# TensorE's program of a spline stage: 32 chunks written out, or a loop over two chunks with its wait counts in registers

## The reference

```
w1b, w2b = sign(w1), sign(w2)
out = relu(batchnorm(conv3x3(x, w1b), gamma1, beta1))
x   = relu(batchnorm(conv3x3(out, w2b), gamma2, beta2) + x)
u = (clip(x * a + b, -1.5, 1.5) + 1) * 0.5 * (K - 1)
i, t = floor(u), u - floor(u)
spline = sum over 4 neighbours of alpha_table[i + k] * basis_k(t)       # R = 8 numbers
out = id_gain * x + einsum('bchwr,cr->bchw', spline, mix) + bias
```

## Time and profile before

| what | value |
|---|---|
| median of 3 runs | 1164.68 us (1160.93 to 1167.83) |
| profiled execution, its own time | 1162.34 us |
| its span, first to last instruction | 1160.5 us |
| mean granted TensorE clock | 0.981 |
| TensorE, weight loads, DVE, ACT busy | 94%, 65%, 82%, 78% |
| first matmul of the spline stage | 445.28 us |
| last 128 matmuls of TensorE (T_LIN and T_VAL of chunk 31) | from 1146.05 us, 5.49 us |

### The profile page before, as it was taken

One profiled execution on the slowest core, in us unless ns is written; L12 is line 12 of the kernel. 1 busy time (PEld: TensorE's weight loads), 2 busy tenths in 40 slices (PEclk: granted clock), 3 DMA queues, 4 the chain that ended last, 5 costly groups with the idle time before them and its releaser, 6 DMA issues.

```text
span 1160.5 us, 51486 instructions
## 1 busy us (share of the span) xinstructions
PE 1093.0 (94%) x23818; PEld 751.4 (65%) x23818; DVE 954.2 (82%) x891; ACT 909.4 (78%) x451; POOL 138.6 (12%) x219
## 2 busy tenths in 40 slices
PE   6999999699999946999999999999999999999996
PEld 4678888578888833665666656665656766665664
DVE  5855656585665777999999999999999999999987
ACT  4435443678788627999999999999999999999971
POOL 7000000058000000011010110110110101101100
PEclk9999999899999977999999999999999999999998
DMA  6766765667767766899999989989999999999652
GB/s 229 260 257 256 278 241 224 229 236 279 278 256 281 289 249 169 189 218 228 220 218 230 218 214 236 220 216 237 215 220 222 213 230 212 225 217 219 147 134 85
DMA packets 58225, 260.95 MB, mean 225 GB/s; under 512 B 16336, under 2 KB 16336, under 8 KB 50000
## 3 DMA queue, kind: packets, MB, share of 16 engines
q1 hardware_dynamic: 48880, 209.20, 55.7%
q0 software_dynamic: 8640, 48.17, 22.7%
q10 hardware_dynamic: 544, 1.10, 0.3%
HBM read 104.29 MB, written 77.07 MB: 156 GB/s over the span
## 4 chain that ended last, share of the span: by engine, by line
PE 60%; DVE 1%; issue 1%; ACTq 0%; ACT 0%; DVEq 0%
PE tab L1161 52%; PE tab L1170 8%; ACTq L949 0%; DVE lin L1120 0%; DVE poly L1116 0%; DVE zbuf L1024 0%; DVE lin L1012 0%; DVE far_sq L1085 0%; DVE poly L1091 0%; DVE middle_mask L1046 0%; ACT zbuf L933 0%; ACT cell L941 0%; DVE lin L1018 0%; DVE offset L1032 0%; DVEq L1084 0%
## 5 line engine op out<-in xcount | busy, mean ns | idle before, releaser
L1161 PE MATMUL tab<-edge_mask,diag 128*32 128x392 bf16 x10240 | 446.8, 329 | 5.9 <-issue 5.9
L1161 PEld LDWEIGHTS tab<-edge_mask,diag 128*32 128x32 f16 x10240 | 277.1, 97 | 168.9 <-issue 28.4
L981 ACT ACTIVATE edge_mask<-cell,thr 128x6272 bf16<-128x6272 bf16 x62 | 338.6, 5508 | 0.5 <-DMA cell<-cell 0.5
L414 ACT ACTIVATE yout<-acc 128x1568 f32<-128x1568 f32 x64 | 94.2, 1472 | 163.0 <-PE acc L715 140.8
L1161 PE MATMUL tab<-middle_mask,diag 128*32 128x392 bf16 x4096 | 186.9, 332 | 26.8 <-DVE middle_mask L1046 22.9
L715 PE MATMUL acc<-band_split,w 64*64 64x392 f16 x4608 | 198.6, 330 | 9.9 <-ACT band_split L372 6.5
L715 PE MATMUL acc<-split,w 64*64 64x392 f16 x4608 | 196.5, 330 | 11.2 <-DVE w L467 9.7
L715 PEld LDWEIGHTS acc<-band_split,w 64*64 64x64 f16 x4608 | 164.3, 107 | 44.0 <-issue 14.8
L715 PEld LDWEIGHTS acc<-split,w 64*64 64x64 f16 x4608 | 154.5, 107 | 52.4 <-issue 11.8
L1161 PEld LDWEIGHTS tab<-middle_mask,diag 128*32 128x32 f16 x4096 | 110.3, 98 | 91.5 <-DVE middle_mask L1046 23.0
L524 DVE BATCH_NORM_STATS2 stats<-yout 128x392 f32 (+1 forms) x240 | 118.0, 555 | 60.8 <-ACT yout L414 60.0
(11 more groups left out here) (133 smaller groups left out, 956.2 us busy)
## 6 DMA issues: line engine op xcount, KB each, us to landing
y_scratch<-yout SPq DMA_DIRECT2D x32, 1568.0 KB, 6.2
cell<-cell SPq DMA_DIRECT2D x504, 98.0 KB, 5.0
xin<-y_scratch SPq DMA_DIRECT2D x16, 1568.0 KB, 9.1
lin<-far POOLq DMA_DIRECT2D x32, 784.0 KB, 9.5
out<-lin SPq DMA_DIRECT2D x31, 784.0 KB, 5.6
xin<-in_x SPq DMA_DIRECT2D x15, 1568.0 KB, 9.3
lin<-y_scratch SPq DMA_DIRECT2D x30, 784.0 KB, 9.5
lin<-in_x POOLq DMA_DIRECT2D x28, 784.0 KB, 7.7
```

Of the source, the lines that this page charges most:

```text
L414: act.activation(yout[b][:, :].rearrange("p (r k x) -> p k r x", r=2, k=TILES)[:, 2 * part:2 * part + 2], acc[:, 4 * part:4 * part + 4, 0: ...
L981: act.activation(mask_of(c, q)[:, :, :], cell4[c % 2][:, :, :], ACT.Sign, bias=thr[:, q:q + 1]).then_inc(sign_mask_ready, 1)
L1161: mm = pe.matmul(tab[(c + t) % 2][j * GROUP:(j + 1) * GROUP, sub, 0:SUB], keep["diag"][part][:, j % 2, t, q, :], mask_of(c, q)[:, j, sub * ...
```

## The change

Only TensorE's program of the spline stage is rewritten. Chunks 0 and 1 are written out, then a loop of 14 rounds runs over two chunks each (an even and an odd one, since the buffers alternate), and chunks 30 and 31 are written out again. The matmuls, their order and the counts they wait for stay the same. In the loop the counts depend on the loop's variable, so they are worked out in registers.

```diff
-            def product(c, t, q, sub):
+            def product(odd, t, q, sub):
+
+                masks = edge_mask[odd][EDGE_QUADS.index(q)] if q in EDGE_QUADS else mask_of(odd, q)
...
             def wait_for_mask(c, q):
 
-                if c == 0:
+                if isinstance(c, int) and c == 0:
                     pe.wait_ge(mask_ready, QUAD_ORDER.index(q) + 1)
                 elif q in EDGE_QUADS:
-                    pe.wait_ge(sign_mask_ready, edge_masks(c - 1) + EDGE_QUADS.index(q) + 1)
+                    pe.wait_ge(sign_mask_ready, len(EDGE_QUADS) * (c - 1) + EDGE_QUADS.index(q) + 1)
                 else:
-                    pe.wait_ge(mask_ready, dve_masks(c - 1) + MIDDLE_QUADS.index(q) + 1)
-
-            def table(c, t):
+                    pe.wait_ge(mask_ready, len(QUAD_ORDER) + len(MIDDLE_QUADS) * (c - 1) + MIDDLE_QUADS.index(q) + 1)
+
+            def table(c, odd, t):
 
                 wait_past(pe, table_used, used(c, t) - 2)
...
-            for c in range(CHUNKS):
-                for t in range(TABLES):
-                    table(c, t)
+            def two_chunks(i):
+                for odd in range(2):
+                    for t in range(TABLES):
+                        table(2 * i + odd, odd, t)
+
+            two_chunks(0)
+            with pe.Fori(1, CHUNKS // 2 - 1) as i:
+                two_chunks(i)
+            two_chunks(CHUNKS // 2 - 1)
```

More of the change, by code:

```diff
@@ L1156, in _ @@
         def _(pe):
-            def product(c, t, q, sub):
+            def product(odd, t, q, sub):
+                masks = edge_mask[odd][EDGE_QUADS.index(q)] if q in EDGE_QUADS else mask_of(odd, q)
                 for part in range(2):
                     for j in range(4):
-                        mm = pe.matmul(tab[(c + t) % 2][j * GROUP:(j + 1) * GROUP, sub, 0:SUB],
+                        mm = pe.matmul(tab[(odd + t) % 2][j * GROUP:(j + 1) * GROUP, sub, 0:SUB],
                                        keep["diag"][part][:, j % 2, t, q, :],
-                                       mask_of(c, q)[:, j, sub * SUB:(sub + 1) * SUB],
+                                       masks[:, j, sub * SUB:(sub + 1) * SUB],
                                        start=(q == QUADS_OF[t][0] and part == 0),
@@ L1166, in product, with add_near_part @@
                 return mm
-            def add_near_part(c, sub):
-                return pe.matmul(tab[(c + T_SQ) % 2][:, sub, 0:SUB], keep["ident"][:, :],
-                                 poly[c % 2][:, sub * SUB:(sub + 1) * SUB], start=False, stop=True)
+            def add_near_part(odd, sub):
+                return pe.matmul(tab[(odd + T_SQ) % 2][:, sub, 0:SUB], keep["ident"][:, :],
+                                 poly[odd][:, sub * SUB:(sub + 1) * SUB], start=False, stop=True)
             def wait_for_mask(c, q):
-                if c == 0:
+                if isinstance(c, int) and c == 0:
                     pe.wait_ge(mask_ready, QUAD_ORDER.index(q) + 1)
                 elif q in EDGE_QUADS:
-                    pe.wait_ge(sign_mask_ready, edge_masks(c - 1) + EDGE_QUADS.index(q) + 1)
+                    pe.wait_ge(sign_mask_ready, len(EDGE_QUADS) * (c - 1) + EDGE_QUADS.index(q) + 1)
                 else:
-                    pe.wait_ge(mask_ready, dve_masks(c - 1) + MIDDLE_QUADS.index(q) + 1)
-            def table(c, t):
+                    pe.wait_ge(mask_ready, len(QUAD_ORDER) + len(MIDDLE_QUADS) * (c - 1) + MIDDLE_QUADS.index(q) + 1)
+            def table(c, odd, t):
                 wait_past(pe, table_used, used(c, t) - 2)
-                if c == CHUNKS - 1 and t == T_VAL:
+                if isinstance(c, int) and c == CHUNKS - 1 and t == T_VAL:
                     for sub in range(4):
                         for q in QUADS_OF[t]:
-                            mm = product(c, t, q, sub)
+                            mm = product(odd, t, q, sub)
                         mm.then_inc(table_ready, 1)
@@ L1198, in table @@
                     for sub in range(4):
-                        mm = add_near_part(c, sub)
+                        mm = add_near_part(odd, sub)
                 mm.then_inc(table_ready, 1)
-            for c in range(CHUNKS):
-                for t in range(TABLES):
-                    table(c, t)
+            def two_chunks(i):
[6 more added lines that the diff above has]
+            two_chunks(CHUNKS // 2 - 1)
 def build(nc, x, w1, w2, par_dram, mix_t, alpha_t, out):
```

## The result

The changed kernel takes 1268.91 us (median of 4 runs, 1265.22 to 1279.12), the kernel before 1164.74 us beside it: 1.091 times as long, 95% interval 1.084 to 1.098, 104 us more.

A forecast was written before the change was run, and what follows sets the result against it. The prediction took TensorE, 94% busy, as the bound. From the profiled 1162.3 us: -13.4 fetch stalls, +62 misses, +8 clock = 1219, forecast 1221 us as a median; 8 in 10 range 1188 to 1315 us.

The forecast's parts named there:

- the likeliest case: Spline loop on TensorE: one missing block per round, 13 times 4.8 us, forecast 1221 us, chance 0.35.
- the second rival: Every block of the spline loop is given up in turn; with two stalls a round median 1295 us, chance 0.25.
- Does the body fit?: The spline loop's 1842 instructions touch 8 blocks, a ninth is fetched too, and nine were taken not to fit.
- That the one given up is the oldest, the loop's first: The ninth block's fetch pushes out the spline loop's first block, giving one miss per round, 62 us in 13.
- The 13.4 us of fetch stalls: TensorE's idle time for late code blocks, chunks 4 to 30 of the spline stage; forecast removed, -13.4 us.
- The price of a miss: At each taken spline-loop branch: 5.7 us latency plus 0.2 branch less 1.1 queued, 4.8 us (1.6 to 7.2).
- The second miss: In the second rival, the next block, 55 instructions after the loop's start, also misses: 4.6 us each, 60 us more.
- The clock: TensorE restarting at half speed after stops: 2.6 us each, 33 us for 13; a quarter counted, 8 us.
- Registers, the moved wait: Spline loop's register operations and the sequencer's own wait for `table_used`: costed at nothing; uncovered, register operations would be 8 us.
- taken branches of the fitting loop: 13 taken branches closing the spline loop on TensorE, at 0.17 us each: +2.2 us.
- The fitting loop: Rival: the spline loop's code stays held and nothing is fetched again; median 1153 us, chance 0.14.

The follow-up runs named there:

- e_less_loop: Changed kernel without the products of T_VAL's low halves: loop body of 1714 instructions touching 7 blocks, no hint; 1146.86 us, ratio 0.985 to the kernel before.
- e_less_slot: As e_less_loop, the same 1714 instructions, but the loop starts 200 instructions into a block and touches 8 blocks; 1262.21 us, ratio 1.083 to the kernel before.
- e_hint: Changed kernel plus one hint instruction per round at the loop's top, naming the closing branch as likely taken; 1154.37 us, ratio 0.992 to the kernel before.
- e_slot0: Changed kernel with the loop's first instruction placed on the edge of a 256-instruction block, still touching 8 blocks; 1257.10 us, ratio 1.079 to the kernel before.
- e_stop_long: e_hint with the loop placed on a block's edge and an empty 16-round loop on TensorE's sequencer ahead of each two chunks; 1260.96 us, ratio 1.083.
- e_once: Changed kernel with its loop replaced by fourteen one-round loops, all chunks written out; wait counts came out as constants; 1161.24 us, ratio 0.998 to the kernel before.
- e_hint_last: e_hint with the hint's outcome read from a register, likely in rounds 1 to 13, unlikely in the last; 1147.85 us, ratio 0.987 to the kernel before.

## Why the prediction came out as it did

The direction was right, and the time lies in the range (1221 us forecast, 1268.9 measured, 1188 to 1315), but the likeliest case was not the one that happened: 56 us more were forecast and 104 came. The range holds the result only because it had been stretched for the second rival. That is partly luck: that rival's 1295 us is near because its second stop was taken far too dear (60 us, measured 18) and its clock too cheap (8 us, measured 29).

*Does the body fit?* Right as argued: eight blocks touched, a ninth asked for, nine too many. e_less_loop and e_less_slot show the limit from both sides, e_hint that the ninth fetch is the cause. The Trainium skill ("Runtime: NRT & Kernel Launch", Instruction fetch mechanics) gives TensorE 2048 instructions in blocks of 256, which is eight; all three runs agree. The same section's sentence that only two blocks are held doesn't: e_less_loop repeats seven without a fetch.

*"That the one given up is the oldest, the loop's first"*: this is the step that failed, in what I let follow from it. I took it that only this one is lost in a round. Nine packets come in every round, so all eight are lost. It was my second rival, the case of two stalls, for which I had 1295 us and a chance of 0.25. That each fetch gives up the oldest block, and so the next one that is needed, explains the nine; that a missing target empties the whole memory would give nine as well, and no run tells the two apart. The 13.4 us of fetch stalls, which the forecast took off, stayed: 12.4 us of idle in place of 9.8.

*The price of a miss.* 4.8 us forecast; measured 53.7 / 13 = 4.1 us of idle, 4.3 in pace. The 5.7 us of latency and 0.2 of branch in it were 5.1 together. This term was mis-sized by little, and the row of one bad block and the share of late ones bracketed it well.

*The second miss.* 4.6 us forecast for that rival, 0.9 us of idle measured, 1.4 in pace; e_slot0 shows that it is one. I had the fetch begin when the loop is entered and take 5.7 us again. In the trace its packet starts 0.8 us behind the end of the branch (592.00, the branch ends at 591.22), where the first miss's starts 2.4 us behind the branch's start, and the matmul behind the second stop starts 2.7 to 3.5 us behind the branch's end. And at half clock the 27 matmuls ahead of it last up to 2.2 us in place of 1.1.

*The clock.* 8 us for the likeliest case. 13 falls came, one at each long stop, and they cost 2.2 us each, 29 us; e_stop_long has 2.3 without any fetch. A quarter of the falls was too few, 2.6 us apiece a little too much: the upper end of 33 us was nearly it.

*The sum by measured terms* is taken from the two traces: the distance of each matmul of the spline stage to the next, less what it is in an undisturbed chunk. 13 x 4.3 (first stop) + 13 x 1.4 (second) + 13 x 2.2 (clock) + 3 (more at the other edges) = 106 us, and the two profiled executions are 1268.1 - 1162.3 = 105.8 us apart. Nothing of the loss is left over.

*Registers, the moved wait.* Nothing, as forecast, which e_hint shows and e_once doesn't. The 2.2 us for taken branches of the fitting loop weren't there either (43.04 us a round).

*The fitting loop.* 1153 us forecast for it; e_hint takes 1154.4 us and has one miss at its end, e_hint_last 1147.9.

## What to carry to other kernels

Count a loop's instructions, and the 256-instruction blocks that they touch from where the loop starts, and add the block behind the end: here TensorE kept eight in all (no run looked at another engine's limit), and one more turned a loop that saves 15 us into one that costs 104. If a body is near that, a hint for its closing branch, or a shift of its start so that it touches a block less, decides it, and the count of code packets in the profile tells at once which side one is on. Before shortening the busiest engine's work, look whether a chain through another engine has the same period. And when a test takes a mechanism apart, look in its trace whether the instructions that it is to test are still there.

## What the runs showed of the hardware that I had not expected

- With nine blocks for eight places every block is fetched again in each round (9 packets), not only the one that is over.
- A hint on the closing branch changes what is fetched ahead: 117 packets fewer, branches of 0.22 us in place of 5.07, and one stop of 4.97 us where the loop falls through, which a hint with a register's outcome removes.
- A missed branch was dearer the nearer it stood behind the last block's edge: 5.1, 6.3 and 6.5 us at 250, 122 and 50 instructions.
- A stop of TensorE of 2.5 us was followed by half clock 9 times of 14 (3.4 us long), one of 5.5 us always (13 of 14 times 6.8 us long), one of 1.45 us not. The fall cost 1.7 us of time where it was 3.4 us long, and 2.3 us on average behind the stops of 5.5 us.
